# Two more dense groups, and a rank read as a maximum, in a two-layer graph kernel on one core

## The reference, cut to what matters

```python
def _L0_gnn_ref(X, edge_index, edge_types, W_data, b_data, W_control, b_control, W_self, b_self):
    Xs = X[src]
    m_data = Xs @ W_data.T + b_data
    m_ctrl = Xs @ W_control.T + b_control
    msg = jnp.where((edge_types == 0)[:, None], m_data, m_ctrl)
    agg = jax.ops.segment_sum(msg, dst, num_segments=X.shape[0])
    return jax.nn.relu(agg + (X @ W_self.T + b_self))

def _L1_gnn_ref(h, d, yes_no, gate_w, gate_b, yes_weight, no_weight, src, dst):
    g = jnp.tanh((h @ gate_w[0, :dim])[dst] + (h @ gate_w[0, dim:])[src] + gate_b[0])
    yn = jnp.tanh(yes_no * yes_weight + (1.0 - yes_no) * no_weight)
    e = (g + yn) * 0.5 * d[dst] * d[src]
    return jax.ops.segment_sum(h[src] * e[:, None], dst, num_segments=n)
...
h = relu(layernorm(x)); x = x + _L0_gnn_ref(h, ...)
h = relu(layernorm(x)); x = x + _L1_gnn_ref(h, ...)
```

## Time and profile before

| what | value |
|---|---|
| time, median of 3 runs | 6099.6 us (6097.68 to 6100.94) |
| span of the profiled execution | 6092.6 us |
| busy share POOL, DVE, PE, ACT | 74%, 69%, 69%, 45% |
| layer 0, its fetches | 123.5 to 2845.0 us |
| layer 1, its fetches | 3106.0 to 5896.5 us |

### The profile page before, as it was taken

The page is one execution under the profiler, slowest core; times in us unless marked ns, Lnnn a source line. Parts: engine busy times, 40 slices in busy tenths (PEclk is TensorE's granted clock), DMA queues, the critical chain, the costliest instruction groups (busy, mean ns, idle before and its releaser), DMA issues.

```text
span 6092.6 us, 113200 instructions
## 1 busy us (share of the span) xinstructions
PE 4187.7 (69%) x28031; PEld 3131.0 (51%) x28031; DVE 4228.4 (69%) x15670; ACT 2756.7 (45%) x9511; POOL 4501.2 (74%) x4524
## 2 busy tenths in 40 slices
PE   6577777777777777765566666666666666666754
PEld 5355555555555555543455555555555555555543
DVE  6877777777777777755366767777776767676763
ACT  5555555555555555533144444444444444444430
POOL 5777777777777777777547777777777777777774
PEclk8588898888989888987688888888888887887775
DMA  7766666666666666666354444444444444444434
GB/s 239 237 198 195 198 191 199 194 194 198 197 193 198 195 192 199 195 199 199 89 135 110 110 111 107 111 110 110 109 111 109 111 110 109 108 110 109 109 95 114
DMA packets 714900, 930.26 MB, mean 153 GB/s; under 512 B 132464, under 2 KB 525716, under 8 KB 713748
## 3 DMA queue, kind: packets, MB, share of 16 engines
q1 hardware_dynamic: 562819, 622.14, 34.5%
q0 software_dynamic: 142848, 297.41, 18.8%
q10 hardware_dynamic: 8592, 3.46, 0.2%
HBM read 862.14 MB, written 60.37 MB: 151 GB/s over the span
## 4 chain that ended last, share of the span: by engine, by line
POOL 71%; issue 23%; PE 2%; DVE 2%; DMA 2%; ACT 0%; SPq 0%; DVEq 0%; ACTq 0%; POOLq 0%
POOL G L569 71%; PE PS L882 1%; PE PS L890 0%; DMA OWF<-in_x 0%; DMA HTB<-ini 0%; DMA G<-t,IDXB 0%; DMA out<-OWF 0%; DVE ST L1169 0%; PE PS L877 0%; DVE OHF L1180 0%; SPq L311 0%; DVE OWF L1188 0%; DVE G L1641 0%; DVE ACC L1487 0%; DVE ACC L1483 0%
## 5 line engine op out<-in xcount | busy, mean ns | idle before, releaser
L569 POOL DMA_INDIRECT G<-t,IDX x4256 | 4216.1, 991 | 1350.2 <-issue 1297.6
L1080 PE MATMUL PS<-CDST,HTB 128*128 128x256 f32 x2092 | 821.2, 481 | 270.7 <-DVE CDST L1770 242.0
L704 ACT ACTIVATE OHF<-PS 128x384 bf16<-128x384 f32 x1568 | 768.5, 490 | 455.3 <-PE PS L926 434.8
L938 PE MATMUL PS<-CDST,OHF 128*128 128x256 bf16 x4704 | 837.4, 291 | 14.4 <-DVE ACC L1280 13.5
L1071 PE MATMUL PS<-HTB,OWF 128*128 128x129 f32 x3136 | 792.2, 341 | 9.1 <-DVE OWF L1749 9.1
L1071 PEld LDWEIGHTS PS<-HTB,OWF 128*128 128x128 f32 x3136 | 689.5, 238 | 170.0 <-issue 87.0
L796 ACT ACTIVATE ST<-PS,MV 128x1 f32<-128x1 f32 x1568 | 407.2, 260 | 581.3 <-issue 237.0
L938 PEld LDWEIGHTS PS<-CDST,OHF 128*128 128x128 bf16 x4704 | 491.6, 105 | 294.5 <-issue 80.3
L899 PE MATMUL PS<-G,OHF 128*32 128x128 f32 x4256 | 219.2, 335 | 600.0 <-DMA G<-t,IDX 553.0
L1080 PEld LDWEIGHTS PS<-CDST,HTB 128*128 128x128 f32 x2092 | 400.7, 238 | 349.9 <-ACT HTB L815 320.4
L899 PE MATMUL PS<-G,OWF 128*32 128x128 f32 x4256 | 227.7, 347 | 481.5 <-DVE OWF L1731 481.5
(11 more groups left out here) (239 smaller groups left out, 8916.7 us busy)
## 6 DMA issues: line engine op xcount, KB each, us to landing
HTB<-t0s SPq DMA_DIRECT2D x392, 384.0 KB
OWF<-t0s SPq DMA_DIRECT2D x392, 384.0 KB
HTB<-t SPq DMA_DIRECT2D x784, 132.0 KB
G<-t,IDX POOLq DMA_INDIRECT x4256
YN<-rows SPq DMA_DIRECT2D x784, 64.0 KB
OHF<-rows SPq DMA_DIRECT2D x784, 64.0 KB
t0s<-HTB SPq DMA_DIRECT2D x25, 384.0 KB
t0s<-OWF SPq DMA_DIRECT2D x24, 384.0 KB
```

Of the source, the lines that this page charges most:

```text
L569: eng.indirect_dma_start(out=G[:, k:k + width], out_offset=None, in_=table, in_offset=bass.IndirectOffsetOnAxis(ap=at, axis=0)).then_inc(s ...
L704: eng.activation(X0[:, k % KX, :, :].rearrange("p n w -> p (n w)"), PS[:, cell_bank(k), 0:384], ACT.Identity).then_inc(q_ev, 1)
L938: ins = eng.matmul(PS[:, 4, 0:DW], X0[:, k % KX, n, :], CD0[:, k % KD, :], start=b == 0 and n == 0, stop=b == NB - 1 and n == 2)
L1080: eng.matmul(PS[:, 4 + g % 2, 0:DW], X1[k % KX1], CD1[k // 2 % 3][:, k % 2, :], start=b == 0, stop=b == NB - 1).then_inc(d_ap, 1)
```

## The change

Two groups of 60 tiles are added to the dense ones, so that `DT` goes from 992 to 1,112, `SM` from 266 to 251, `NCT` from 124 to 139, and the cells of a layer from 1,568 to 1,764. The rank no longer takes a product and a sum. The triangle's diagonal is set to 16384 (`OWNED`), which adds that number to an edge's count in its own block and in no other, and the maximum over the blocks is 16384 plus the rank. The constants that the rank is compared with are shifted by the same number.

```diff
-RUNS = ((16, 62),)
+RUNS = ((16, 62), (2, 60))
...
+OWNED = 16384
...
-        JB = SRD[:, NB:3 * NB].bitcast(bf16)
...
-            eng.iota(IO16[:, :], pattern=[[1, 2 * DW]], base=0, channel_multiplier=0).then_inc(s_k, 1)
+            eng.iota(IO16[:, 0:DW], pattern=[[1, DW]], base=0, channel_multiplier=0).then_inc(s_k, 1)
+            eng.iota(IO16[:, DW:2 * DW], pattern=[[1, DW]], base=OWNED, channel_multiplier=0).then_inc(s_k, 1)
...
+            eng.scalar_tensor_tensor(TRI[:, 0, :], IDENT[:, :], float(OWNED), TRI[:, 0, :],
+                                     ALU.mult, ALU.add).then_inc(s_k, 1)
...
-                    eng.wait_ge(q_rk, q - KO + 1)
...
-                if q >= 1:
-                    eng.wait_ge(q_rr, q)
-                eng.tensor_tensor(JB[:, 0:n * NB], PS[:, 5 + q % 2, 0:n * NB], OHBQ[q % KO][:, 0:n * NB],
-                                  ALU.mult).then_inc(q_rk, 1)
+                eng.tensor_reduce(RANKS[:, g % 2, j:j + n],
+                                  PS[:, 5 + q % 2, 0:n * NB].rearrange("p (a w) -> p a w", w=NB),
+                                  mybir.AxisListType.X, ALU.max).then_inc(q_rk, 1)
                 eng.wait_ge(q_rk, q + 1)
-                eng.tensor_reduce(RANKS[:, g % 2, j:j + n], JB[:, 0:n * NB].rearrange("p (a w) -> p a w", w=NB),
-                                  mybir.AxisListType.X, ALU.add).then_inc(q_rr, 1)
-                eng.wait_ge(q_rr, q + 1)
...
-                                      IO16[:, 0:128].unsqueeze(1).broadcast_to([128, 2, 128]),
+                                      IO16[:, DW:DW + 128].unsqueeze(1).broadcast_to([128, 2, 128]),
...
-                eng.tensor_scalar(RANKS[:, g % 2, :], RANKS[:, g % 2, :], 128.0, None, ALU.is_ge, ALU.max,
+                eng.tensor_scalar(RANKS[:, g % 2, :], RANKS[:, g % 2, :], float(OWNED + 128), None, ALU.is_ge, ALU.max,
```

More of the change, by code:

```diff
@@ L284, in gnn_program @@
             "q_b", "q_p", "q_tri", "q_rk", "q_r", "q_tab", "q_te", "q_dec")
-        q_o, q_rr, q_gf, q_tr, q_row, q_rs = sems("q_o", "q_rr", "q_gf", "q_tr", "q_row", "q_rs")
+        q_o, q_gf, q_tr, q_row, q_rs = sems("q_o", "q_gf", "q_tr", "q_row", "q_rs")
         q_ot, q_oh, q_ga, q_ev, q_ap, q_z = sems("q_ot", "q_oh", "q_ga", "q_ev", "q_ap", "q_z")
@@ L909, in _ @@
             eng.wait_ge(a_se, NC)
-            eng.wait_ge(s_k, 5)
+            eng.wait_ge(s_k, 7)
             for n in range(2):
@@ L1124, in _ @@
             eng.tensor_copy(IOTA[:, :], IOI[:, :])
-            eng.wait_ge(s_k, 2)
+            eng.wait_ge(s_k, 3)
             link(eng.tensor_copy(PIF[:, :], PIO[:, :]))
@@ L1131, in _ @@
             eng.wait_ge(s_c, 5)
-            eng.wait_ge(s_k, 4)
+            eng.wait_ge(s_k, 5)
+            eng.scalar_tensor_tensor(TRI[:, 0, :], IDENT[:, :], float(OWNED), TRI[:, 0, :],
+                                     ALU.mult, ALU.add).then_inc(s_k, 1)
             halves = IDENT[:, :].rearrange("p (q h w) -> p q h w", h=2, w=W)
```

## The result

The changed kernel takes 5831.78 us (median of 4 runs, 5828.93 to 5835.68) against 6099.99 us before: the ratio is 0.9557, with a 95% interval of 0.9544 to 0.9571. It was forecast at 5812 us, with a range of its own of 5780 to 5830 and of up to 5900 with a small form of the first two rivals.

A forecast was written before the change was run, and what follows sets the result against it. POOL's fetches, one after another, were taken to bound the kernel. Removing fetches saves 310.8 us, less 23 us of stretch: 288 us off 6099.6 gives 5812 us, range 5780 to 5830, up to 5900 with smaller first two rivals.

The forecast's parts named there:

- the first two rivals: PE becomes the bound in layer 0, 5940 us, chance 0.12; DVE becomes the bound in layer 1, 5937 us, chance 0.05.
- POOL as the bound, before and after: Both layers: POOL's fetches one after another set the time; 120 fewer in each layer save 310.8 us together.
- The cost of the added cells, nothing: Both layers: 196 more cells each cost nothing; PE at most 9.70 of 10.23 us an item, DVE 9.20 of 10.49.
- The last rival but one: TensorE's clock falls in layer 0, an item takes 16 us at 1.2 GHz: 7200 us, chance 0.02.
- The first rival: PE becomes the bound in layer 0 at 10.8 us an item, losing 128 us: 5940 us, chance 0.12.
- The rank's product, worth nothing by itself: DVE's rank work: dropping a 0.54 us product per unit saves no time, since DVE is not the bound.
- DMA: Layer 0: table-block loads grow by a fifth, giving 225 GB/s; costed at nothing.
- The stretch of the fetches: DVE's work lengthens POOL's fetches: 5 us in layer 0, 18 us in layer 1; +23 us, between 0 and 34.
- The middle and the end: Sections and middle stage stay as before; costed at nothing.
- The port rival: Shared DVE/GpSimd port holds POOL for whole cell instructions in layer 1, +234 us instead of 18: 6028 us, chance 0.03.
- What was to be seen: Signs of being right: fetches every 1.28 and 1.32 us, shorter PE and DVE waits, layer 0's last fetch near 2700 us.

The follow-up runs named there:

- Two edits: Changed kernel with layer 1's target one-hots, or its pair one-hot, as scalar_tensor_tensor: 5815.66 and 5832.84 us alone, 5739.84 us together.

## Why the prediction was right, point by point

*POOL as the bound, before and after.* Right. POOL's idle time is "issue" in both kernels, and the 120 fetches fewer in each layer are where the time went.

*The cost of the added cells, nothing.* Right for 18 groups, and the room was as thin as said. PE's way through an item of layer 0 is 10.25 - 0.96 = 9.29 us, where 9.5 to 9.7 was the bound, and the granted clock rose from 0.89 to 0.95, so a part of the way went with the slow clock. The last rival but one, a clock that falls, is refuted by that. DVE's way in layer 1 is 10.62 - 1.95 = 8.67 us against a bound of 9.20. The first rival, PE in layer 0, was real but two groups away: the kernel with 20 groups shows it, at the 10.8 us an item that the rival had named.

*The rank's product, worth nothing by itself.* Right: a ratio of 1.0009 alone. The price taken for the reduce from PSUM, 0.55 us, was 0.544.

*DMA.* Right: 223 GB/s where 225 was worked out, without effect.

*The stretch of the fetches, +23 us between 0 and 34.* This is the mis-sized term. In layer 0 it was 2 ns, as taken. In layer 1 it was 17 ns, or 34 us over 2,008 fetches, where I had taken 9 ns (18 us) and had thought 12 ns the most. The step that failed is "if all of it grew as the cells do, it would be 63 x 0.192": the stretch is not a share of DVE's time. It is the chance that a fetch starts under a DVE instruction that holds it, times what is left of that instruction, and both grew. In the rows of 4000 to 5000 us, fetches held by the target one-hot went from 87 of 765 to 104 of 755, about as the cells grew, but each was held for 279 ns instead of 262; all held fetches together went from 43% to 54% of the row, at 142 and 144 ns. The size is not exact: run again, the changed kernel had 980 and 1030 ns, 5 and 23 ns more than before, so the 2 ns of layer 0 agree with the prediction's 2.6 in part by luck.

*The middle and the end.* Costed at nothing; they and the start took 5.6 us. With the 16 us of the stretch of layer 1 that makes up for most of the 23.5 us by which the span fell short of the 288 us forecast.

*The port rival, 6028 us.* Wrong in its size, right in its mechanism, which I had not expected. I had argued from an average of 0.5 us an item that ordinary instructions hold a fetch hardly at all. They do hold it, for up to 0.5 us, but only when it starts under them, and for their rest alone. The trace of before already has it: 328 of its 765 fetches of 4000 to 5000 us take over 15 ns more than 943, 142 ns more on average, which the mean of 63 ns a fetch had hidden.

*What was to be seen.* The last fetch of layer 0 at 2701 us (near 2700); PE's wait 0.96 us (0.5 to 0.9) and DVE's 1.95 us (1.3 to 1.8), both a little above what was said, as it would be if scaling the whole item asks too much of the other engines; a fetch of layer 1 every 1.328 us (1.32).

## What to carry to other kernels

Where an engine is the bound by its own instructions one after another, moving work off it to others is worth those instructions, less what the moved work stretches the rest by (here 41 of 311 us), as long as the longest way of any other engine through a step, its stalls included and its wait for the bound left out, stays under the bound's. The way of the changed kernel, 9.3 us, scaled by the added work, gave 10.9 us an item for 20 groups, where 10.79 was measured. Instructions saved on an engine with spare time buy nothing. And an indirect DMA's issue time is not a constant: look at what DVE runs at the moment where each one starts. The means of a stage hide it, and the single starts show it. One DVE instruction written as two shorter ones of another kind, with the same result, was worth some 76 us, more than a quarter of what the whole change brought.

## What the runs showed of the hardware that was not expected

A fetch that starts with DVE idle takes 943 ns. One that starts 0.10 us or more behind the start of a tensor_tensor, scalar_tensor_tensor or tensor_scalar on SBUF operands takes as much longer as is left of that instruction, less 0.13 us (2,497 of 2,498 cases), whatever the kind. One that starts with L1768 or just before it is not held (77 fetches, 8 ns more on average), nor is one under the tensor_reduce L1706 (33 fetches). Two edits that took 12 and 10 ns off a fetch alone took 55 off together, because with both most fetches started on the seams between DVE's instructions. TensorE's granted clock in layer 0 rose with the work on it, from 0.89 to 0.95 and 0.99 (19 groups), while PE's wait for landings fell from 2.13 to 0.96 and 0.38 us an item.
